# A graph kernel on one core: SyncE copies 54 columns of gathered rows, one row at a time

## The reference

```
edge_index = stack([src, dst])
h = maximum(layernorm(x), 0);  x = x + L0(h, edge_index, ...)
h = maximum(layernorm(x), 0);  x = x + L1(h, edge_index, edge_attr_64, ...)
h = maximum(layernorm(x), 0);  x = x + L2(h, edge_index, ...)
h = maximum(layernorm(x), 0);  x = x + L3(h, edge_index, edge_weight, ...)
```

## Time and profile before

| | |
|---|---|
| median of 3 runs | 11408.42 us (11405.88 to 11408.51) |
| the profiled execution | 11410.4 us, its span 11408.5 us |
| busy | POOL 8190.2 us, DVE 7216.0, ACT 5413.3, PE 956.1 |
| queue q1 (issued by SP) | 459776 packets, 28.0% of 16 engines |
| queue q0 (issued by POOL) | 331904 packets, 24.9% of 16 engines |

### The profile page before, as it was taken

One profiled execution on the slowest core, in us unless ns is written; L12 is line 12 of the kernel. 1 busy time (PEld: TensorE's weight loads), 2 busy tenths in 40 slices (PEclk: granted clock), 3 DMA queues, 4 the chain that ended last, 5 costly groups with the idle time before them and its releaser, 6 DMA issues.

```text
span 11408.5 us, 38369 instructions
## 1 busy us (share of the span) xinstructions
PE 956.1 (8%) x3312; PEld 677.7 (6%) x3312; DVE 7216.0 (63%) x6971; ACT 5413.3 (47%) x6326; POOL 8190.2 (72%) x8632
## 2 busy tenths in 40 slices
PE   4122222221000000030000001100000000000001
PEld 3111111110000000010000000000000000000001
DVE  8845555553888888869999997454444543333334
ACT  6244444442666666546766765333333333333332
POOL 2177777777777777667777776777777767777776
PEclk8555565555555555565555555555555555555555
DMA  8756666663666666546666665333333333333333
GB/s 307 275 193 204 202 206 200 204 202 109 215 211 216 210 216 211 198 148 224 223 222 226 220 226 160 96 110 113 110 113 111 112 96 103 107 103 106 106 104 97
DMA packets 792030, 1943.01 MB, mean 170 GB/s; under 512 B 214034, under 2 KB 425962, under 8 KB 791369
## 3 DMA queue, kind: packets, MB, share of 16 engines
q1 hardware_dynamic: 459776, 1126.04, 28.0%
q0 software_dynamic: 331904, 814.65, 24.9%
q10 hardware_dynamic: 144, 0.41, 0.0%
HBM read 1201.70 MB, written 738.73 MB: 170 GB/s over the span
## 4 chain that ended last, share of the span: by engine, by line
POOL 61%; issue 24%; DVE 7%; DMA 4%; ACT 2%; PE 1%; POOLq 0%; SPq 0%; DVEq 0%; ACTq 0%
POOL region L1382 58%; DMA region<-x,ix_s 2%; DVE psR L1513 2%; POOL work L1808 1%; DVE region L656 1%; DVE region L657 1%; DVE psB L1430 1%; DVE work L1528 1%; DVE psR L1521 0%; ACT work L1622 0%; POOL start_rows_by_dst L1136 0%; POOL start_ed L972 0%; DMA region<-h,ix_s 0%; POOL start_rows_by_src L1131 0%; PE psR L759 0%
## 5 line engine op out<-in xcount | busy, mean ns | idle before, releaser
L1528 DVE TENSOR_TENSOR_SCAN work<-work,psR 128x1792 f32<-128x1792 f32 (+2 forms) x496 | 1971.3, 3974 | 92.5 <-DVE ix_s L1449 56.5
L1382 POOL DMA_INDIRECT region<-x,ix_s x1612 | 1521.2, 944 | 502.3 <-issue 460.7
L1382 POOL DMA_INDIRECT region<-qm,ix_s x1612 | 1524.0, 945 | 492.6 <-issue 490.1
L1382 POOL DMA_INDIRECT region<-kv,ix_s x1612 | 1524.1, 945 | 491.0 <-issue 484.3
L1382 POOL DMA_INDIRECT region<-k,ix_s x1612 | 1521.5, 944 | 491.2 <-issue 490.9
L1382 POOL DMA_INDIRECT region<-h,ix_s x1612 | 1521.4, 944 | 491.2 <-issue 488.8
L1546 ACT COPY work<-region 128x1664 f32<-128x1664 f32 (+1 forms) x496 | 1162.2, 2343 | 1307.2 <-DMA region<-start_rows_by_dst 775.4
L1430 DVE TENSOR_TENSOR_SCAN psB<-psB,work 128x1792 f32<-128x1792 f32 (+1 forms) x496 | 1485.1, 2994 | 397.8 <-ACT psB L1559 350.8
L1622 ACT COPY work<-work 128x1664 f32<-128x1664 f32 (+2 forms) x496 | 1539.2, 3103 | 0.0
L1621 ACT COPY psR<-work 128x128 f32<-128x128 f32 (+2 forms) x496 | 189.3, 382 | 2463.9 <-DVEq L1529 2463.9
L1458 DVE TENSOR_TENSOR work<-region,psB 128x1664 f32<-128x1664 f32 x372 | 702.1, 1887 | 808.9 <-DMA region<-k,ix_s 528.2
(11 more groups left out here) (339 smaller groups left out, 5050.9 us busy)
## 6 DMA issues: line engine op xcount, KB each, us to landing
region<-start_rows_by_dst SPq DMA_DIRECT2D x248, 832.0 KB, 6.8
state_p<-work SPq DMA_DIRECT2D x124, 936.0 KB, 4.9
state_p<-work SPq DMA_DIRECT2D x124, 884.0 KB, 3.8
region<-start_rows_by_src SPq DMA_DIRECT2D x124, 832.0 KB, 9.9
start_rows_by_dst<-zero_t SPq DMA_DIRECT2D x62, 1664.0 KB, 7.7
state_pA<-work SPq DMA_DIRECT2D x124, 832.0 KB, 4.9
state_p<-work SPq DMA_DIRECT2D x124, 832.0 KB, 3.5
start_rows_by_src<-zero_t SPq DMA_DIRECT2D x1, 59904.0 KB, 163.6
```

The lines of the kernel that those rows point to most:

```text
L1382: g_.indirect_dma_start(to[b][:, k, 0:wd_s], None, q.tabs, bass.IndirectOffsetOnAxis(ap=ix_s[b][:, k:k + 1], axis=0))\
L1528: c.do(nc.vector.tensor_tensor_scan(q.st[:, 0:F * (K + 1)], decay_at(q, b)[:, 0:F * (K + 1)], summed[:, 0:F * (K + 1)], 0.0, ALU.mult, ALU ...
```

## The change

In the passes PA, P1, P2 and P3, the last column of the second half of some pairs is no longer gathered by POOL. SP copies its 128 rows, one DMA for each row, from the pass's table to a table `rows_ahead` in DRAM, and later loads that column from there into the half's buffer with one DMA. In P1 and P3 (`OFTEN`) this is one column in every 4 pairs, 15 in a pass; in PA and P2 (`SELDOM`) one in every 5 pairs, 12 in a pass. Together these are 54 columns and 54 x 128 = 6912 row copies. The copies of one column are spread over 4 (or 5) pairs, that is 32 (or 25 to 26) rows in a pair, half of them in each half, behind that half's near load and ahead of its store. The column is brought in at the pair that follows.

The row numbers of these columns are copied by DVE, turned by PE and cast by ACT into `numbers_i` (27 partitions of 128 numbers) ahead of PA. At the start of each pair SP loads that pair's 32 (25 to 26) numbers into registers. POOL's loop is written out over 4 (or 5) pairs. DVE waits for `column_in` ahead of the half that uses such a column, and the semaphores that count the gathers are shared by the passes.

```diff
+            def pair(i, short):
                 for b in range(2):
                     g_.wait_ge(*q.on(f"free{b}", i + 1))
                     if q is P1:
                         g_.wait_ge(q.own(f"next{b}"), i + 1)
                     g_.sem_inc(S("pool_go"), 1)
-                    for k in range(K):
+                    for k in range(K - (short and b)):
                         g_.indirect_dma_start(to[b][:, k, 0:wd_s], None, q.tabs, bass.IndirectOffsetOnAxis(ap=ix_s[b][:, k:k + 1], axis=0))\
...
-                v.wait_ge(q.own(f"rows{b}"), i * (16 * K) + 16 * K)
+                v.wait_ge(*q.rows(b, gathered(q, i, b)))
+                if brought(q, i, b):
+                    v.wait_ge(S("column_in"), 16 * (column_number(q, columns_ahead(q, i) - 1) + 1))
...
+        def numbers_dve(v):
+            for h in (OFTEN, SELDOM):
+                nc.vector.tensor_copy(numbers_f[:, h.at:h.at + h.cols], oth_i[1][:, h.col:T:2 * K * h.pairs]).then_inc(S("numbers"), 1)
+        def numbers_pe(pe):
+            pe.wait_ge(S("numbers"), 2)
+            nc.tensor.transpose(numbers_ps[0:NUMBERS, :], numbers_f[:, :], ident[:, :]).then_inc(S("numbers"), 1)
+        def numbers_act(act):
+            act.wait_ge(S("numbers"), 3)
+            nc.scalar.copy(numbers_i[:, :], numbers_ps[0:NUMBERS, :]).then_inc(S("numbers"), 1)
...
+        def row_ahead(sp, q, j, r, number):
+            wd = q.tabs.shape[1]
+            sp.dma_start(ahead_t[j, r:r + 1, 0:wd], q.tabs[bass.ds(number, 1), :]).then_inc(S(f"row_ahead{column_number(q, j) % 2}"), 16)
+        def numbers_of(q, j, a, z):
+            return nc.values_load_multi_w_load_instructions(numbers_i[q.ahead.at + j:q.ahead.at + j + 1, a:z], engines=(mybir.EngineType.SP,), min_val=0, max_val=PADN,
+                                                            skip_runtime_bounds_check_because="a row number is the number of a node, at most PADN")[1]
+        def column_in_sp(sp, q, j):
+            wd = q.tabs.shape[1]
+            c = column_number(q, j)
+            sp.wait_ge(S(f"row_ahead{c % 2}"), (c // 2 + 1) * 16 * P)
+            sp.wait_ge(*q.on("free1", q.ahead.first + j * q.ahead.pairs + 1))
+            sp.dma_start(gathered_rows(q)[1][:, K - 1, 0:wd], ahead_t[j, :, 0:wd]).then_inc(S("column_in"), 16)
...
+            if q.ahead:
+                sp.wait_ge(S("numbers"), 4)
+                for nm in q.needs:
+                    sp.wait_ge(S(nm[0]), nm[1])
             def two(i, last):
                 if q is PB:
                     zeros_chunk_sp(sp, i)
+                j = i // q.ahead.pairs if q.ahead else 0
+                fetch = q.ahead and j < q.ahead.cols
+                if fetch:
+                    a, z = part_of(q, i)
+                    numbers = numbers_of(q, j, a, z)
                 for b in range(2):
                     if not last and q.near is not None:
                         sp.wait_ge(*q.on("made", i * 6 + (3 * b + 1)))
                         near_load(sp, q, i + 1, b)
+                    if brought(q, i, 1) and not b:
+                        column_in_sp(sp, q, columns_ahead(q, i) - 1)
+                    if fetch:
+                        mid = (a + z) // 2
+                        for r in (range(a, mid), range(mid, z))[b]:
+                            row_ahead(sp, q, j, r, numbers[r - a])
                     if not last and q is P1:
                         sp.wait_ge(S(f"bias_used{b}"), i + 1)
                         bias_load(sp, i + 1, b)
```

More of the change, by code:

```diff
@@ L165, in graph_layers_kernel @@
         head = sb("head", [P, D])
+        numbers_f = sb("numbers_f", [P, 27])
+        numbers_i = sb("numbers_i", [27, P], I32)
+        numbers_ps = psB[:, 3, 256:256 + P]
         bias2 = [sb(f"bias2_{o}", [P, P]) for o in range(2)]
@@ L297, in graph_layers_kernel, with __init__ @@
         psrow_src = [stat[:, :, :, :].rearrange("p j a h -> p (j a h)")[:, b * K * 12:(b + 1) * K * 12] for b in range(2)]
+        class Ahead:
+            def __init__(self, pairs, at):
+                self.pairs, self.at = pairs, at
+                self.cols = (IT // 2 - 2) // pairs
+                self.first = pairs + 1
+                self.col = self.first * 2 * K + 2 * K - 1
+                assert 2 + pairs * self.cols == IT // 2 and at + self.cols <= NUMBERS
+        NUMBERS = 27
+        OFTEN, SELDOM = Ahead(4, 0), Ahead(5, 15)
         keys_dram = dram("keys_in", [2, P, C])
@@ L311, in graph_layers_kernel @@
         x3_t = dram("x3", [NN * P, D])
+        ahead_t = dram("rows_ahead", [OFTEN.cols, P, 264])
         keyrow_t = [dram(f"keyrow{o}", [P, T], I16) for o in range(2)]
@@ L335, in own, with gathers, rows @@
                 return S(f"{self.name}_{what}")
+            def gathers(self, b):
+                return K * (IT // 2) - (self.ahead.cols if self.ahead and b else 0)
+            def rows(self, b, value):
+                i = passes.index(self)
+                return S(f"rows{b}_{i % 3}"), value + sum(16 * q.gathers(b) for q in passes[i % 3:i:3])
             def total(self, what):
@@ L363, in graph_layers_kernel @@
         passes = [PB, PA, P1, P2, P3]
+        AHEAD = {PA: SELDOM, P1: OFTEN, P2: SELDOM, P3: OFTEN}
         for q in passes:
+            q.ahead = AHEAD[q] if q in AHEAD else None
+        for q in passes:
+            q.ahead_before = sum(p.ahead.cols for p in passes[:passes.index(q)] if p.ahead)
             q.bv, q.abig, q.st, q.psrow, q.zt, q.prod = bv, abig, st, psrow, zt, prod
@@ L1374, in pass_pool @@
                 g_.indirect_dma_start(head[:, 0:q.HF], None, q.tabd, bass.IndirectOffsetOnAxis(ap=head_i[q.o][:, 0:1], axis=0)).then_inc(q.s("head_in"), 16)
-            with g_.Fori(0, IT // 2) as i:
+            def pair(i, short):
                 for b in range(2):
@@ L1380, in pass_pool, with columns_ahead, brought, gathered @@
                     g_.sem_inc(S("pool_go"), 1)
-                    for k in range(K):
+                    for k in range(K - (short and b)):
                         g_.indirect_dma_start(to[b][:, k, 0:wd_s], None, q.tabs, bass.IndirectOffsetOnAxis(ap=ix_s[b][:, k:k + 1], axis=0))\
-                          .then_inc(q.own(f"rows{b}"), 16)
+                          .then_inc(q.rows(b, 0)[0], 16)
+            if q.ahead:
+                pair(0, False)
+                pair(1, False)
+                n = q.ahead.pairs
+                with g_.Fori(0, q.ahead.cols) as j:
+                    for u in range(n):
+                        pair(j * n + (u + 2), u == n - 1)
+            else:
+                with g_.Fori(0, IT // 2) as i:
+                    pair(i, False)
+        def columns_ahead(q, i):
+            return max(0, (i - 1) // q.ahead.pairs)
+        def brought(q, i, b):
+            return q.ahead and b and i >= q.ahead.first and (i - q.ahead.first) % q.ahead.pairs == 0
+        def gathered(q, i, b):
+            return 16 * (K * (i + 1) - (columns_ahead(q, i) if q.ahead and b else 0))
         def heads(t, q):
@@ L1660, in near_load, with column_number, part_of @@
                          q.near[0:EP, :].rearrange("(p t) w -> p (t w)", t=T)[:, bass.ds(i * (2 * K * q.HF) + b * K * q.HF, K * q.HF)]).then_inc(q.s(f"near_in{b}"), 16)
+        def numbers_dve(v):
[7 more added lines that the diff above has]
+            nc.scalar.copy(numbers_i[:, :], numbers_ps[0:NUMBERS, :]).then_inc(S("numbers"), 1)
+        def column_number(q, j):
+            return q.ahead_before + j
+        def row_ahead(sp, q, j, r, number):
[10 more added lines that the diff above has]
+            sp.dma_start(gathered_rows(q)[1][:, K - 1, 0:wd], ahead_t[j, :, 0:wd]).then_inc(S("column_in"), 16)
+        def part_of(q, i):
+            n = q.ahead.pairs
+            return P * (i % n) // n, P * (i % n + 1) // n
         def pass_sp(sp, q):
@@ L2193, in _ @@
             v.sem_inc(S("edges_ready"), 1)
+            numbers_dve(v)
             pass_dve(v, PA)
@@ L2223, in _ @@
             carry_act(act, PB)
+            numbers_act(act)
             pass_act(act, PA)
@@ L2249, in _ @@
             carry_pe(pe, PB)
+            numbers_pe(pe)
             carry_pe(pe, PA)
```

## The result

| | before | after |
|---|---|---|
| median | 11406.27 us (9 runs, 11404.79 to 11410.51) | 11437.10 us (9 runs, 11433.46 to 11442.86) |
| profiled execution, span | 11410.4, 11408.5 us | 11441.4, 11439.5 us |

The changed kernel takes 1.0027 times as long (95% interval 1.0018 to 1.0036): 31 us slower where 62 us faster was forecast. It lies 7 us above the upper end of the range.

What follows compares the result with a forecast made beforehand. POOL's gather issue, about 1.25 us each, was taken as the bound. Removed gathers -67.5, DVE's number copies +0.3 and P1's charge +5 gave -62.2 us: from 11410.4 to 11348.2 us, range 11337 to 11430.

Steps and rivals of the forecast that it cites:

- The loading of the numbers: SP at each pair's head, ahead of the near load: estimated 2.0 us, making ACT 0.21 us late per P1 pair.
- L: Time SP takes to load one pair's row numbers into registers, estimated at 2.0 us.
- The late near rows: Rival in P1: a longer number load delays the near load ACT awaits; 11452 us at a 4.0 us load, chance 0.15.
- its formula: P1's lengthening in us: 60 x (number load - 1.79) - 42.5, set against the 48.7 us gain of the other three passes.
- This clearing: PA: number load free up to 6.4 us, from ACT's 2.7 us and DVE's 3.7 us a pair.
- the prediction's signs of being wrong: POOL in P1 waiting for late buffers, L1546's start moving over 3 us in first halves, or SP's store later than the sums.
- The copies: SP's row copies: 0.55 us each, 17.6 us a P1 pair, all hidden in SP's idle time.
- charged 5 us of its 18.75: P1: 5 us loss assumed, between nothing and all 18.75 us of its removed gathers, because cover is uneven between pairs.
- P1 gains nothing, the others all: Rival: DVE and ACT take back P1's 18.75 us through transfers landing later beside the copies; 11362 us, chance 0.15.
- an issue slowed by the copies: Rival on POOL: 1% on the gathers' pitch costs 78 us, giving 11420; chance 0.09, shared with partial mixes within 0.2%.
- SP's overrun in P1: Rival: at 0.88 us a copy an SP pair takes 33.6 us, 1.1 over the 32.5 before; 11428 us, chance 0.06.

Runs made afterwards that it cites:

- The aligned parts' run: Changed kernel with the parts of a column beginning at multiples of four numbers (24 or 28 rows a pair in PA and P2): 11371.3 us, 0.9962 of the kernel before.
- the loads alone: Changed kernel with POOL gathering every column, one unread copy a pair left, number loads still ahead of the near load: 11470.6 us, 1.0043 of the kernel before.
- the kernel with both causes taken away: Changed kernel with the number load behind the near load and 256 instead of 264 floats copied in PA: 11358.1 us, 0.9944 of the kernel before.
- the kernel that skips the gathers: Changed kernel without number loads or row copies; POOL skips 54 gathers, SP brings in the table's first 128 rows: 11355.0 us, 0.9940 of the kernel before.

## Why the prediction was wrong

**The step that failed** is "The loading of the numbers": L = 2.0 us, "by the row of one and add two thirds". It measured 3.6 us in P1 and 7.2 in PA (the median; 36 of 60 loads long). The step had placed the load on the right spot and had named its threshold, 3.3 us, beyond which the change isn't faster. The value was chosen from a gap of 1.23 us, and the prediction said that no row shows a load alone, though the trace of before holds the instruction itself, among the few that SP runs at its branches:

```profile
L587 SPq TENSOR_LOAD <-flag_i x4: 287/480/904, 490.2 to 4835.2; - x4
```

0.29 us for one number, the shortest of four, would have said that 26 numbers fetched one after another take 7.5 us, over twice the threshold. PA's long loads took 7.2. The closeness is partly luck: the median of the four, 0.48, would have said 12.5. The aligned parts' run shows that alignment halves the load. Why is open. My reading was that aligned numbers are fetched in groups of four, and the two or one left over singly: 24 aligned numbers took 3.5 us, 25 3.7 and 26 4.1, which fits. But 28 took 3.5 to 3.7 and 32 in P1 3.6, hardly more than 24, so the number of groups doesn't price a load.

**The late near rows** were the slower rival, priced for P1 alone: 11452 at L = 4.0, and by its formula 11410.4 - 48.7 + 66 = 11428 at the 3.6 us that P1's loads took. The changed kernel measured 11437. The mechanism was right, and that the number is near is luck, because the formula puts all of it on P1: there the loads alone cost 14 us and not 66, and PA, which I had cleared up to L = 6.4 by adding ACT's 2.7 us to DVE's 3.7 us a pair, lost 67 us against its forecast. This clearing is the second step that failed. By it the loads alone, with no gather removed, were to cost PA about 25 us (36 long ones of 7.3, less 6.6); they cost 46. My reading is that the sum of a pass's waits can't be drawn on as one account: a near load that is late by 7 us comes in one half, and in that run the first half of a long pair took 18.3 us instead of 16.25.

Of P1 the same run shows why it was overpriced: a near load that goes out away from the store lands sooner. In the pair shown above, ACT starts on the near rows 6.9 us after the issue beside the store (3103.31 to 3110.24), and 4.4 us after the late one (3126.58 to 3130.94). Over the passes the medians are 6.8 and 4.6 us in PA, and 6.9 and 5.2 in P1. So P1's near load goes out 3.65 us later and its rows are there only 2.0 us later, against the 1.79 us that ACT has to spare; in PA 7.3 us become 5.0, against 2.7. With that PA shows two of the prediction's signs of being wrong, which it had looked for in P1: the near rows over 3 us late, and SP's store later than the sums. In P1 the third came: POOL waits 33.0 us for buffers given back, against 6.7 before.

**The copies** were sized at 0.55 us, and measured 0.67 and 0.92. In P1, P2 and P3 this stayed hidden, as forecast. In PA 7.2 + 12.0 + 0.9 = 20.1 us don't fit a half of 16.25. I had compared SP's work with a pair (18 us of 32.5). With the measured prices a pair with a long load needs 7.2 + 26 x 0.92 + 1.8 = 33 us of 32.5, one with a short load 29.6, and over five pairs it just holds (31.6 of 32.25). It is the half with the long load that doesn't. The same 20.1 us stand in P2, where SP waited for the sums only 73.0 us in the whole pass, and P2 lost nothing: ACT and DVE have 6 us a half to spare there, against 2.7 and 1.9 in PA. So an overfull half seems to cost only where the slack behind it is smaller than the lateness; no run changed the slack by itself.

**P1** was charged 5 us of its 18.75, and keeps 11.2 back even with neither loads nor copies on SP. The rival "P1 gains nothing, the others all" was half right, but for another reason than late transfers: 0.23 us of the 0.34 us wait covered a gap of DVE's own, and the rest in part DVE's wait for ACT (14 us more in the pass). The other 16 us that P1 lost are due to the place of the load: they came back when it went behind the near load.

**What held:** 1.25 us for each gather removed, in full in P2 and P3; that POOL's pitch doesn't notice the copies (1992.5 us over 1596 intervals in P3 are 1.2484 us, against 1.2483 before); next to no wait for the columns brought in (2.6 us in 5 halves); near nothing between the passes (4 us, 0.3 forecast). The rival of an issue slowed by the copies falls with this, and so does SP's overrun in P1: its first half of 3.6 + 10.6 + 1.9 us just fits 16.25.

## What to carry to other kernels

When an idle engine is given work, don't compare the work with its idle sum: find what the engine next issues that others wait for, and compare the work ahead of each such issue with the slack of that one half. Before estimating an instruction from a gap, ask the trace for the instruction itself, the sequencers' own included. And a wait that one means to use up may cover another wait; what can be had is the part above it.

## What the runs showed of the hardware

- One instruction that loads 25 or 26 numbers of 4 bytes into registers took 6.9 to 7.7 us where it began at a place in its row that isn't a multiple of 16 bytes, and 3.5 to 4.2 us where it began at one. 24 or 28 numbers at a multiple of 16 bytes took 3.2 to 3.8 us, 32 took 3.6 in P1 and 3.3 in P3 (medians). The first load of a pass was shorter (1.5 to 2.1 us). Beside a near load the median of PA's loads was 7.9 us instead of 7.2.
- A DRAM to DRAM copy of one row is issued in 0.49 us with 128, 144, 256 or 272 floats and in 0.70 to 0.73 with 132 or 264. The Trainium skill ("DMA: Bandwidth & Descriptors", section "Why a DMA increments its semaphore by 16 and not by 1") says that a DMA issued this way runs on the largest number of engines up to 16 that divides the slowest dimension of both sides, that a contiguous row can be split for it by software, and that the issuing sequencer itself writes to the semaphore what is missing to 16. 264 and 132 divide by 12 and not by 16, and the longer issue agrees. So do the packets of queue q1: the kernel with both causes taken away, whose PA copies have 256 floats instead of 264, has 676448 against the changed kernel's 664160. That is 8 more for each of 1536 copies, as 16 parts instead of 12 give if each part has a packet of data and one for the semaphore. Whether the missing writes are what makes the issue longer, no run shows.
- On the chip where the kernel before took 12791 us, the loads alone took 12806, 15 us more where it was 64 on the other chip, and the kernel that skips the gathers 12687 to 12723 in three of its four runs. The kernel with 256-float copies behind the near load took 15155 to 15409 in its four runs; there SP's register instruction of 37 ns took up to 1.9 us. PB, which the change doesn't touch, took 2389 us in that run instead of 2011. Why was not looked into. This kernel with a nearly full SP lost far more on that chip than the other two did.
